# A decoder layer in fp32 on one core: the feed-forward weights' blocks are prepared one attention turn earlier, and the first pair of groups enters the feed-forward part from inside the last attention turns

## What is computed

```python
x = x + ssm(layernorm(x))                      # a state-space step along the batch axis
x = x + cross_attention(layernorm(x), ctx)     # 16 heads of 32, 77 context tokens
h = layernorm(x) @ W_exp + b_exp               # 512 -> 2048
h = butterfly(h, up_weights)                   # 11 stages of 2x2 mixes over 2048
h = gelu(h + up_bias)
h = butterfly(h, down_weights)
x = x + h @ W_con + b_con + down_bias          # 2048 -> 512
```

## Time and profile before

| | us |
|---|---|
| median of 3 runs | 2365.08 (2363.87 to 2365.98) |
| the profiled execution's own time | 2366.6 |
| its span in the trace | 2364.8 |
| PE busy | 2226.1 (94%) |
| PE's weight loads busy | 1943.3 (82%) |
| DVE busy | 1769.8 (75%) |
| ACT busy | 1293.1 (55%) |
| POOL busy | 557.2 (24%) |
| mean granted clock of PE | 0.971 |

### The profile page before, as it was taken

How to read it: one execution, slowest core, us unless ns; L and a number is a source line. 1 busy time by engine, 2 the same in 40 slices (tenths; PEclk the granted TensorE clock), 3 DMA queues, 4 the chain that set the end, 5 groups by cost and what they waited for, 6 DMA issues and landing times.

```text
span 2364.8 us, 42243 instructions
## 1 busy us (share of the span) xinstructions
PE 2226.1 (94%) x15752; PEld 1943.3 (82%) x15752; DVE 1769.8 (75%) x2969; ACT 1293.1 (55%) x2832; POOL 557.2 (24%) x619
## 2 busy tenths in 40 slices
PE   8877789999999999969999999999999999999998
PEld 4777668778777877748998998988989989989898
DVE  5999668878878887755875867857858758678567
ACT  2998556666667666543644635535536446355343
POOL 3788222222222322200030030020210300300203
PEclk9888879999999999989999999999999999999999
DMA  8555702332332232256568677676685686776765
GB/s 329 192 178 189 263 2 77 116 124 77 108 116 94 85 119 90 95 182 219 172 219 267 199 218 227 208 262 179 212 263 177 214 266 200 223 221 210 225 188 177
DMA packets 190883, 424.47 MB, mean 179 GB/s; under 512 B 27342, under 2 KB 64718, under 8 KB 190286
## 3 DMA queue, kind: packets, MB, share of 16 engines
q1 hardware_dynamic: 190696, 421.94, 55.1%
HBM read 331.29 MB, written 90.60 MB: 178 GB/s over the span
## 4 chain that ended last, share of the span: by engine, by line
PE 65%; DVE 16%; ACT 11%; issue 4%; DMA 3%; POOL 1%; SPq 0%; DVEq 0%; ACTq 0%; POOLq 0%
PE ps L416 52%; PE ps L1805 5%; ACT es L982 5%; PE ps L1773 2%; DVE gl L1178 2%; DVE G L1530 2%; DVE st L1149 2%; DVE ptl L1178 1%; DVE wc_s L1178 1%; PE ps L1784 1%; DMA xa<-in_x 1%; DVE rsum L1401 1%; ACT wc_h L939 1%; DVE rmax L1390 1%; ACT pth L957 1%
## 5 line engine op out<-in xcount | busy, mean ns | idle before, releaser
L416 PE MATMUL ps<-ring,gh 128*128 128x256 f32 x3584 | 654.4, 285 | 12.6 <-DVE gl L1178 12.5
L416 PEld LDWEIGHTS ps<-ring,gh 128*128 128x128 f32 x3584 | 558.0, 192 | 16.9 <-DVE gl L1178 15.7
L416 PE MATMUL ps<-xth,ring 128*128 128x512 f32 x1792 | 554.6, 390 | 4.2 <-ACT U L1066 4.2
L416 PE MATMUL ps<-ring,gl 128*128 128x256 f32 x1792 | 506.8, 283 | 0.0
L416 PEld LDWEIGHTS ps<-xth,ring 128*128 128x128 f32 x1792 | 337.4, 188 | 74.7 <-issue 4.6
L1054 ACT ACTIVATE gh<-G 128x512 fp32r<-128x512 f32 x384 | 237.2, 629 | 212.4 <-PE ps L416 212.1
L416 PE MATMUL ps<-xtl,ring 128*128 128x512 f32 x896 | 349.5, 390 | 0.0
L416 PEld LDWEIGHTS ps<-ring,gl 128*128 128x128 f32 x1792 | 343.4, 192 | 0.0
L1178 DVE TENSOR_TENSOR gl<-G,gh 128x512 fp32r<-128x512 f32 x384 | 278.8, 739 | 57.2 <-ACT gh L1054 55.6
L759 POOL TENSOR_TENSOR es<-es,rinv 128x308 f32<-128x308 f32 x256 | 180.2, 735 | 456.5 <-DVE rinv L1405 456.5
L1470 DVE TENSOR_TENSOR U<-ps,U 128x512 f32<-128x512 f32 (+1 forms) x168 | 137.3, 817 | 169.5 <-PE ps L416 166.9
(11 more groups left out here) (212 smaller groups left out, 4646.0 us busy)
## 6 DMA issues: line engine op xcount, KB each, us to landing
ring<-wup_scratch SPq DMA_DIRECT2D x224, 512.0 KB, 3.8
ring<-wdn_scratch SPq DMA_DIRECT2D x224, 512.0 KB, 3.6
X<-x_scratch SPq DMA_DIRECT2D x32, 1024.0 KB, 8.5
xa<-in_x SPq DMA_DIRECT2D x16, 1024.0 KB, 5.5
x_scratch<-xa SPq DMA_DIRECT2D x16, 1024.0 KB, 4.3
x<-x_scratch SPq DMA_DIRECT2D x16, 1024.0 KB, 5.6
x_scratch<-x SPq DMA_DIRECT2D x16, 1024.0 KB, 4.3
out_x<-X SPq DMA_DIRECT2D x16, 1024.0 KB, 6.3
```

What stands on the lines that cost most here:

```text
L416: mm = pe.matmul(bank, a, b, start=first and i == 0, stop=last and i == n - 1, skip_group_check=go_on)
```

## The change

It has six parts.

1. Block `g` of the weights is made in turn `g`, for `g` = 0 to 15, instead of block `g-1`. In turns 1 to 15 the same instructions stand in the same places. Block 0 is new in turn 0: mixed after the maxima of tile 3, split behind `exp(3)` on ACT and beside `sums(3)` on DVE. Turn 16 makes none.
2. SP's queue: within an iteration of the loop, `store_wc(g - 1)` and `load_wc(g)` come before `turn(g)`. With part 1 the low parts for which `store_wc(g - 1)` waits are made at the end of turn `g-1`; before, at the end of turn `g`. At the end of the queue, the store of block 14 and the load of block 15 come before the loads of `X`.
3. The moments of the first pair's groups are taken in turn 15: the spread of group 0 behind the shift of tile 0, its moments behind `sums(0)`; group 1 the same at tile 2. POOL takes the deviations behind its division of tiles 0 and 2.
4. ACT norms group 0 in turn 15 behind `high_weights`, and group 1 in turn 16 behind `hi_p(2, -1)`.
5. PE transposes the first pair in turn 16 in two fours, one behind `project(2, -2)` and one behind `project(3, -2)`; the order is `FIRST_TURN`, so that the first four need group 0 alone.
6. In turn 16 the seven operands are split among the values' splits instead of behind them.

```diff
+        FIRST_TURN = 0, 1, 4, 5, 2, 3, 6, 7
...
             for g in range(2, NG - 2):
                 b = g // GB
-                turn(g)
                 store_wc(g - 1)
                 load_wc(g)
+                turn(g)
...
+            store_wc(NG - 3)
+            load_wc(NG - 2)
             store_x2(NG - 2)
+            store_wc(NG - 2)
+            load_wc(NG - 1)
             sp.wait_ge(pe_slot, SLOTS * (NG - 1))
             load_x2(0)
             load_x2(1)
-            store_wc(NG - 3)
-            load_wc(NG - 2)
             store_x2(NG - 1)
-            store_wc(NG - 2)
-            load_wc(NG - 1)
+            store_wc(NG - 1)
             store_x2(NG)
-            store_wc(NG - 1)
             sp.wait_ge(wc_stored, 32 * NG)
...
                     mul.then_inc(p_ready, 1)
+                    if g == NG - 1 and t == 0:
+                        rsqrt(2 * NG, xn2_ready, NG)
+                    if g == NG - 1 and t == 2:
+                        rsqrt(2 * NG + 1, xn3_ready, 1)
...
                 hi_p(2, -1)
+                if g == NG:
+                    apply3(1)
+                    for i in range(4):
+                        raw_x(0, i, i, FIRST_TURN[i])
                 hi_p(3, -1)
+                if g == NG:
+                    for i in range(4, 8):
+                        raw_x(0, i, i - 4, FIRST_TURN[i])
                 exp(0)
...
                     load_table(ACT.Gelu)
-                    apply3(0)
+                    act.wait_ge(x2_stored, 16 * (NG - 2))
+                    act.wait_ge(wc_stored, 32 * NG)
+                    hi_x3(0, B11)
+                    hi_x3(0, T3)
                 hi_v(0)
                 hi_x(0)
                 if g == NG:
-                    apply3(1)
+                    hi_x3(0, T2)
                 exp(1)
                 hi_v(1)
                 hi_x(1)
+                if g == NG:
+                    hi_x3(0, B21)
                 hi_v(2)
                 hi_v(3)
-                if 1 <= g <= NG:
-                    high_weights(g - 1)
+                if 1 <= g < NG:
+                    high_weights(g)
+                if g == NG - 1:
+                    apply3(0)
...
                 exp(3)
+                if isinstance(g, int) and g == 0:
+                    high_weights(0)
...
                 shift(0)
+                if g == NG - 1:
+                    spread3(0)
                 lo_p(3, -1)
                 sums(0)
+                if g == NG - 1:
+                    moments(2 * NG)
                 residual(3, -2)
                 if g == NG:
-                    stats3(1)
+                    split_first(0, 2)
+                    mix_x(0, 1)
                 if g == NG + 1:
-                    split_first(5, PROD)
+                    split_first(6, PROD)
                 shift(1)
                 lo_v(0)
                 lo_x(0)
-                if 1 <= g <= NG:
-                    mix_weights(g - 1)
+                if 1 <= g < NG:
+                    mix_weights(g)
+                if g == NG:
+                    lo_x3(0, T2)
                 sums(1)
                 lo_v(1)
                 lo_x(1)
+                if g == NG:
+                    split_first(3, 4)
                 lo_v(2)
                 lo_v(3)
                 if g == NG:
-                    low_weights(g - 1, 0)
-                    low_weights(g - 1, 1)
+                    split_first(4, 5)
...
                 shift(2)
+                if g == NG - 1:
+                    spread3(1)
...
                 sums(2)
+                if g == NG - 1:
+                    moments(2 * NG + 1)
                 lo_x(3)
-                if g == NG:
-                    split_first(0, 3)
                 residual(1, -1)
                 if g == NG:
-                    split_first(3, 5)
+                    split_first(5, 6)
                 lo_p(1, 0)
                 shift(3)
+                if isinstance(g, int) and g == 0:
+                    mix_weights(0)
                 lo_q(0)
-                if 1 <= g < NG:
-                    low_weights(g - 1, 0)
+                if 0 <= g < NG:
+                    low_weights(g, 0)
                 sums(3)
-                if 1 <= g < NG:
-                    low_weights(g - 1, 1)
+                if 0 <= g < NG:
+                    low_weights(g, 1)
...
                 project(2, -2)
+                if g == NG:
+                    pe.wait_ge(e_ready, T * NG)
+                    pe.wait_ge(exp_ps, T * NG)
+                    for i in range(4):
+                        turn3(0, FIRST_TURN[i], i)
                 scores(0)
                 turn_p(3, -1)
                 project(3, -2)
+                if g == NG:
+                    for i in range(4):
+                        pe.wait_ge(x3_raw, i + 1)
+                        turn3(0, FIRST_TURN[4 + i], i)
```

More of the change, by code:

```diff
@@ L760, in norm @@
                     mul.then_inc(p_ready, 1)
+                    if g == NG - 1 and t == 0:
+                        rsqrt(2 * NG, xn2_ready, NG)
+                    if g == NG - 1 and t == 2:
+                        rsqrt(2 * NG + 1, xn3_ready, 1)
             attn_loop(pool, norm)
-            rsqrt(2 * NG, xn2_ready, NG)
-            rsqrt(2 * NG + 1, xn3_ready, 1)
             tt = nc.gpsimd.tensor_tensor
@@ L924, in apply3, with raw_x @@
                 apply(xs, xs, xn3_ready)
-            def raw_x(p, i, bank):
+            def raw_x(p, i, bank, to=None):
                 act.wait_ge(x3_pe, 8 * p + i + 1)
@@ L929, in raw_x @@
                     act.wait_ge(t1_mixed, HC * (p - 1) + i + 1)
-                A(rawx[:, i // 2, i % 2, :], ps[:, bank, :], ACT.Copy).then_inc(x3_raw, 1)
+                to = i if to is None else to
+                A(rawx[:, to // 2, to % 2, :], ps[:, bank, :], ACT.Copy).then_inc(x3_raw, 1)
             def hi_x3(p, o):
@@ L1003, in attn_act @@
                 hi_x(1)
+                if g == NG:
+                    hi_x3(0, B21)
                 hi_v(2)
                 hi_v(3)
-                if 1 <= g <= NG:
-                    high_weights(g - 1)
+                if 1 <= g < NG:
+                    high_weights(g)
+                if g == NG - 1:
+                    apply3(0)
                 if g == NG:
-                    for i in range(8):
-                        raw_x(0, i, i % 4)
-                    act.wait_ge(x2_stored, 16 * (NG - 2))
-                    act.wait_ge(wc_stored, 32 * NG)
-                    for o in SPLIT_ORDER:
+                    for o in SPLIT_ORDER[4:]:
                         hi_x3(0, o)
@@ L1301, in _, with spread3 @@
                 sub(ql[:, c, :], ps[:, 4 + c, :], qh[:, c, :]).then_inc(pre_lo, 1)
-            def stats3(g):
+            def spread3(g):
                 dve.wait_ge(x2_loaded[g % 2], 16 * (g // 2) + 16)
-                stats(2 * NG + g, X[:, g % 2 * T:(g % 2 + 1) * T])
+                spread(X[:, g % 2 * T:(g % 2 + 1) * T], range(T)).then_inc(ln_step, 1)
             def mix_weights(n):
@@ L1410, in attn_dve @@
                 residual(2, -2)
-                if g == NG:
-                    stats3(0)
                 shift(0)
+                if g == NG - 1:
+                    spread3(0)
                 lo_p(3, -1)
                 sums(0)
+                if g == NG - 1:
+                    moments(2 * NG)
                 residual(3, -2)
                 if g == NG:
-                    stats3(1)
+                    split_first(0, 2)
+                    mix_x(0, 1)
                 if g == NG + 1:
-                    split_first(5, PROD)
+                    split_first(6, PROD)
                 shift(1)
@@ L1733, in turn3 @@
             def turn3(p, i, bank):
-                pe.wait_ge(xn3_ready, 2 * p + 2)
+                pe.wait_ge(xn3_ready, 2 * p + (2 if p else 1 + i // 2 % 2))
                 grp, f = i // 2 % 2, i // 4 * 2 + i % 2
@@ L1834, in attn_pe @@
                 values(3)
-                if g == NG:
-                    pe.wait_ge(e_ready, T * NG)
-                    pe.wait_ge(exp_ps, T * NG)
-                    for i in range(4):
-                        turn3(0, i, i)
                 turn_p(0, 0)
@@ L1844, in attn_pe @@
                 turn_x(3)
-                if g == NG:
-                    for i in range(4):
-                        pe.wait_ge(x3_raw, i + 1)
-                        turn3(0, 4 + i, i)
                 project(1, -1)
```

## The result

The changed kernel took 2352.42 us (median of 6 runs, 2350.10 to 2357.06), the one before 2364.69 us beside it (6 runs, 2363.67 to 2366.07). The ratio is 0.9945, with the 95% interval [0.9934, 0.9955]: faster by 12.3 us. The forecast was 2347.6.

The account below looks back on a forecast made before the run. PE was taken to set the time (65% of the chain), with DVE (16%) where it keeps PE waiting. Gains of 14.4 + 0 + 1.4 + 1.7 = 17.5 us took 2365.1 to 2347.6 us; range 2339.5 to 2355.5.

Parts of the forecast that it names:

- step 1: SP's queue: values' loads go out in mid-turn, removing PE's stalls and slow clocks in turns 5, 9, 13; gain 14.4 us.
- Step 2: Turn 0: block 0's added mixing and splits fit DVE's idle time; 0 us, at most 4.1 us of DVE.
- Step 3: Turn 15: DVE waits 3.2 us for X; PE reaches tile 3's transposes 8.7 us later, plus 2.0 for slow clocks.
- the rival with the slower landing: Group 0 of X lands after 9.7 us, not 5.8, so DVE waits 3.9 us more: 2351.5 us; chance 0.10.
- Step 4: Turns 16 and 17: tile 3's transposes to A12 in 41.6 us instead of 53.7, with a new PE stall of 6.2.
- Step 5: Behind A12: PE's clock no longer runs at 0.63 for the first 4.6 us; gain 1.7 us.
- the new stalls don't come: Rival: X lands in time (3.2 us) and the clock holds (4.8 us), giving 2339.6 us; chance 0.12.
- The rival of slow clocks: PE's clock falls behind each new gap, on the path, 3 x 3.0 us instead of 2.0 + 2.8: 2351.8; chance 0.15.
- its 2.85 us: PE's gap in turn 15 before the change, with clock at 1.00 over 985.80 to 992.00, cited against the skill's rule.

Follow-up runs that it names:

- statistics later: Changed kernel with spread, moments and POOL's deviation of X's first group one tile later in turn 15: 2342.92 us, ratio 0.9906.
- parts 1 and 2 alone: Kernel before with only blocks one turn earlier and SP's queue as changed; statistics, norms, transposes and splits unmoved: 2345.00 us, ratio 0.9918.
- value first: Changed kernel with the first value's high and low parts in turn 16 ahead of operand T3's: 2352.09 us, ratio 0.9936.
- norm later: Changed kernel with ACT's norm of group 0 in turn 15 behind tile 0's high parts: 2350.52 us, ratio 0.9931.
- table early: Changed kernel with ACT's GELU table load in turn 16 ahead of the last four copies of X: 2353.51 us, ratio 0.9946.
- values late: Changed kernel with keys' and values' loads at a change of batch back behind the next block's store and load: 2366.30 us, ratio 1.0005.
- `X` first: Changed kernel with group 0 of X loaded ahead of block 14's store, group 1 behind block 15's load: 2344.22 us, ratio 0.9915.
- all four edits: Changed kernel with `X` first, norm later, table early and value first together: 2342.16 us, ratio 0.9899.
- the fastest version: Changed kernel with all four edits and statistics later together: 2340.41 us, ratio 0.9891.

## Why the prediction was right

The sign and the range held: 2352.42 lies in 2339.5 to 2355.5. The point was 4.8 us too fast. In the profiled pair the sum was 17.5 us against 14.95. Nearly all of the gain is step 1; of the 3.1 us that steps 3 to 5 were to bring, the pair shows 0.3.

- **Step 1, SP's queue, 14.4 us: right.** 14.6 at turn 14's mark; the kernel with this alone gained 14.0 in the medians of its job, and the change without it nothing.
- **Step 2, turn 0, nothing: right.** DVE's idle time before the first query's low part went from 3.67 to 2.25 us, with that instruction 0.1 us later instead of 1.4, and PE's idle times in turns 0 and 1 are the same (2.55 and 3.20).
- **Step 3, turn 15, 8.7 us plus 2.0 of clock: the mechanism right, the size not.** Tile 3's transposes came 13.3 us later against the turns' gain (1007.68 + 14.6 - 1008.94), so 2.6 more than the two terms. The mechanism was as told: DVE was free at 959.7, 14.6 us before the 974.3 of the text, and waited; PE idled before the values and before `project(0)`, the latter 3.61 us against 3.5. But "*the faster of the two landed after 5.8 us*" was a row of two loads with no transfer of their own queue in front; here they went out right behind a block's load, and group 0 took 7.7. And the block's store took 7.7 us (948.85 to 956.57) up to its successor's load, where the one I had read, in the quiet of turn 16, took 7.1. So the wait was 5.9 us and not 3.2, and PE's first idle time 6.44 and not 3.8. That is halfway to the rival with the slower landing (9.7 us), which would have given 2351.5. The 7.7 us is itself no fixed price: with the same transfers in the same order in front, the first of the two loads took 6.4, 7.9, 8.1, 8.1, 8.6 and 9.0 us in six other traces (statistics later, parts 1 and 2 alone, value first, norm later, table early, values late).
- **Step 4, from there to A12 in 41.6 us: right,** 41.85 (1049.53 - 1007.68), with the new stall of 6.16 us where the text had 6.2. (Its last terms add up to 1059.0, not 1059.2, which changes nothing.)
- **Step 5, clock behind A12, 1.7 us: right,** 1.8 (1302.2 - 1300.4).

**What the sum hid.** It added steps 3 and 4 to -3.4, for the whole change, and never asked what parts 1 and 2 would give without the rest. Had it done so, the wait for `X` that part 3 brings would have stood alone as a cost, beside a block that leaves turn 16 for nothing. The runs show it as 6 to 9 us by the ratios: 2345.0 without parts 3 to 6, 2352.4 with them, 2344.2 and 2342.9 with them and no wait. Of the rival "*the new stalls don't come*", for which I had 2339.6, those last two fulfil only the first half: `X` is there in time, but the idle times of 3.6 us before `project(0)` (3.35 in the second) and of 6.2 us before `values(2)` are still there, with half clock behind the former (0.50 over 979.0 to 983.0 with `X` first). Taking that one wait away was worth 7 to 9 us by the ratios, where the text priced it at 3.2 and all slow clocks together at 4.8.

The rival of slow clocks (2351.8) is next to the measured time, and partly true: the granted clock fell behind the idle time before the values (0.57 over 966 to 974) and the new stall (0.62 over 1021 to 1030), as it did at the batch stalls before. Yet the profiled pair does not need it: the late landing and the longer store (1.9 + 0.6) are as large as its 2.6 us. The other 2.3 us of the miss lie in the medians: the sum was taken off the kernel before as 1.5 us below its profiled execution, and the changed kernel's median is 0.8 above its own. What makes this kernel's times spread over 7 us, and those of all four edits over 1.1, is open. The traces offer two things that vary: the landing of `X`, which took 7.7 to 9.0 us in the five traces in which DVE waited for it, and the clock behind short idle times.

The rule on the clock gate in the Trainium skill ("TensorE: Matmul & The Clock Gate", on HAM oscillation) is that idle gaps, if they are long enough, bring half rate, and that PE has to warm up again behind each. It agrees with three of the waits here (8.38 and 4.51 us in the kernel of parts 1 and 2, 6.16 us in the changed one). It does not settle the short ones, and the prediction was wrong to hold its 2.85 us against it. These went both ways: half clock behind 1.96 us (statistics later, 0.53) and 2.70 us (all four edits, 0.50 over 970.2 to 973.2), full clock behind 1.97 us (the fastest version), 2.71 us (`X` first) and 2.85 us (the kernel before). So in these traces the length of a short gap does not tell whether the clock falls, and what does is open.

## What to carry to other kernels

When a change has several parts, price the parts as if each came alone: here one moved queue entry gave as much as the whole change, the blocks' earlier turn some 7 us more (by the medians of one job, 4.5 by the ratios, whose intervals overlap), and the other four parts took that back through a single wait. Before you move a reader of a DMA'd tile earlier in an in-order queue, find when the data lands with the new neighbours in front of it, not when it landed alone; everything behind the reader pays. The cure was small here: the reader one tile later, or its load one transfer earlier. The second has a price, since the load delays what is now behind it: the next block's load could be issued only 4.5 us later, which DVE felt (3.73 us) in the one kernel with no statistics ahead of its mixing.

## What the runs showed of the hardware that was not expected

In these traces a transfer pays for what stands ahead of it in its queue, and hardly for what stands behind. Where group 0 of `X` (1 MB) is issued just ahead of a block's store of 2 x 896 KB, the next block's load could be issued only 11.5 to 11.7 us after the store's second half, in all four kernels that have this order. SP's queue of the one with all four edits and the statistics later:

```profile
951.86 0.37 SPq L606 DMA_DIRECT2D X<-x_scratch  x1
952.27 0.57 SPq L587 DMA_DIRECT2D wdn_scratch<-wc_h  x1
952.88 0.67 SPq L588 DMA_DIRECT2D wdn_scratch<-wc_s  x1
964.50 1.22 SPq L579 DMA_DIRECT2D wc_s<-wd_scratch  x2
```

Without `X` ahead it was 7.1 us (949.45 to 956.57 in the changed kernel; the 7.7 us of step 3 count from the first half), so 1 MB in front cost the store some 4.5 us. The load in front took 6.4 to 6.5 us to land in these four kernels, with the store right behind it, and 5.8 in the kernel before, with the other load of `X` behind it. With `X` first the three landed in the order of their issue: `X` at 956.2 (949.65 + 6.5), the store's halves at 960.0 and 962.3 (950.06 + 9.9, 950.67 + 11.6). The kernel before shows it too, with both groups of `X` ahead (its SP queue): 13.3 us.

```profile
966.04 0.92 SPq L605 DMA_DIRECT2D X<-x_scratch  x2
967.00 0.56 SPq L586 DMA_DIRECT2D wdn_scratch<-wc_h  x1
967.61 2.94 SPq L587 DMA_DIRECT2D wdn_scratch<-wc_s  x1
980.89 1.22 SPq L578 DMA_DIRECT2D wc_s<-wd_scratch  x2
```

Those rows stood in the trace that the forecast was made from. Read for what a neighbour in front does to a transfer, they would have said that `X`, behind a block's load, would hardly land in the 5.8 us that it took in front of everything. How much later they would not have said: the seven traces with this order have 6.4 to 9.0 us.
